# Masking the scores of a causal linear attention: one engine for all 16 heads, or three engines for two halves

## Chip, cores and metric

One core of a Trainium2 chip. The metric is the time of one execution on the device in microseconds (us), the median of several runs.

## What is computed

The program is one transformer-like chain on `x` of 2 x 2048 tokens with 128 channels in float32: a landmark attention, a feed-forward part with blockwise FP4 rounding (FFN), a causal linear attention, and the same FFN again. Each has a layer norm ahead of it and a residual sum behind it. Only the linear attention is touched. Cut to what matters, for 16 heads of 8 channels:

```
q, k = elu(q) + 1, elu(k) + 1
for every token t:                      # a scan over the 2048 tokens
    kv   += k[t] (x) v[t]
    ksum += k[t]
    y[t]  = (q[t] @ kv) / (q[t] . ksum + 1e-6)
out = y @ W_proj + b_proj
```

## The kernel before

The 4096 tokens are 32 tiles of 128 tokens, and four tiles make a quad (`QD = 4`). The scan is done in blocks. In a tile, the part of the same 128 tokens is a product of 128 x 128 scores for each head, masked to the upper triangle, with the values (`lin_scores`, mask, `lin_attend`). The part of all tokens before it comes from a running state of 128 x 128 (`lin_state_mm` on TensorE, `lin_state` on VectorE).

`lin_scores(n)` (line 1488) makes all heads of tile n in four matmuls of 32 rows by 512 columns, one for each group of 32 rows of the array (`r` = 0 to 3), each into a PSUM bank of its own: banks 1 to 4 (`SCORE_BANK = 1`). Banks 1 and 2 hold heads 0 to 7, banks 3 and 4 heads 8 to 15. There is one set of these four banks. The masked scores have two buffers, `masked[n % 2]`.

Before the change the two halves go different ways. VectorE masks heads 0 to 7 straight from PSUM by a product with a triangle of ones (`lin_mask`, line 1091). ScalarE copies heads 8 to 15 out of PSUM unmasked to a buffer `raw` (`lin_raw`, line 698), and POOL, which reads only SBUF in this kernel, selects the triangle from `raw` into `masked` (`lin_select`, line 406). `lin_attend(n)` (line 1507) waits for both halves, and `lin_scores(n + 1)` waits until banks 1 and 2 are masked and, ahead of its third matmul, until banks 3 and 4 are copied out.

Each quad needs front work ahead of its tiles: transposes (`lin_transposes`, 1448), the q and k products (1454, 1455), exponentials (679, 682), caps on POOL (396), the two feature maps on VectorE (`lin_phi`, 1045 and 1049), the v product and the transpose of k, a running sum of k on VectorE (`lin_scan`, 1058), its product with q on POOL (`lin_qk`, 401), the denominators (`lin_den_mms` on TensorE, 1471; `lin_den` on VectorE, 1073 and 1077), their spread (692) and transpose (1478), and the scaled, block-diagonal q on VectorE (`lin_qbd`, 1082 and four instructions of 1085). `lin_scores` of a quad's first tile waits for its `lin_qbd`.

The order is written out by hand. Iteration n of the loop on each engine holds the steps of tile n, the scores and the mask of tile n + 1, and one quarter of the front work of quad q = (n + 1) / 4 + 1, by `phase = (n + 1) % 4`:

- TensorE: scores(n + 1); phase 0 transposes, 1 q and k products, 2 v product, 3 transpose of the denominators; attend(n); state_mm(n); in phase 2 den_mms; proj(n).
- VectorE: out(n - 1); mask(n + 1); stats(n - 1); phase 3 qbd, 1 phi, 2 scan and v; state(n); in phase 2 den.
- ScalarE: raw(n + 1); phase 0 xbT, 1 exps, 2 pk; yT(n); phase 3 norm of the quad after; in phase 2 spread.
- POOL: select(n + 1); phase 1 the caps, 2 qk, 3 bias.

The front work of seven quads (1 to 7) lies in this loop; that of quad 0 lies in the FFN before it. Behind tiles 28 to 31 each engine also does the first steps of the second FFN (`LIN_FILL`: `step1(-4)` to `step1(-1)`). Every engine works its own list in order and stops at a wait.

Of the kernel before, what the change touches and what calls it, by code (L numbers as in the profile page):

```python
# [16 lines left out]
ALU = mybir.AluOpType  # L17
ACT = mybir.ActivationFunctionType
AX = mybir.AxisListType.X

P = 128
B, N = 2, 2048
NT = N // P
TILES = B * NT
# [26 lines left out]
QW = QD * P  # L51
# [6 lines left out]
FRONT_A, FRONT_B, SCORE_BANK, STATE_BANK, NUM_BANK = 7, 0, 1, 5, 6  # L58
# [6 lines left out]
def build(nc, x_d, wqkvT_d, band_d, wfc_d, bfc_d, wattn_d, battn_d, wproj_d, bproj_d,  # L65
          wg_d, wu_d, wd_d, eye_d, scaled_eye_d, tri_d, blockmask_d, headones_d, rowhead_d, valid_d, centre_d, out_d):
    with ExitStack() as ctx:
# [9 lines left out]
        s = Signals()  # L77

        def need(eng, name, value):

            if not (isinstance(value, int) and value <= 0):
                eng.wait_ge(s[name], value)
# [17 lines left out]
        def part(n):  # L100
            used[0] += n
            return arena[:, used[0] - n:used[0]]
# [67 lines left out]
        tri = xn_store[:, 6 * P:7 * P]  # L170
# [7 lines left out]
        phq, phk, kcum, qn = ([part(QW) for _ in range(2)] for _ in range(4))  # L178
        pk = [part(QW).rearrange("p (k c) -> p k c", c=P) for _ in range(2)]
        masked = [part(HB * P).rearrange("p (h t) -> p h t", t=P) for _ in range(2)]  # L180
        raw = part(2 * QW)
        den, rden = (part(QD * HB).rearrange("p (k h) -> p k h", h=HB) for _ in range(2))
        rdenB = part(QW)
        state, ynT = ([part(P) for _ in range(2)] for _ in range(2))
# [2 lines left out]
        ps = ctx.enter_context(nc.psum_tensor("ps", [P, 8, 512], F32))  # L187
        psf = ps[:, :, :].rearrange("p a b -> p (a b)")
# [42 lines left out]
        def lin_states(n):  # L231

            return n - n // NT if n > 0 else 0
# [58 lines left out]
        def _(g):  # L292
            tt = nc.gpsimd.tensor_tensor
# [47 lines left out]
            def layernorm_moments(p, q):  # L341

                g.wait_ge(s["stats_done"], p * TILES + (q + 1) * QD)
                tiles = slice(q * QD, (q + 1) * QD)

                def const(k):
                    return lnc[:, k:k + 1].broadcast_to([P, QD])

                steps = ((0, mv[:, tiles, 1], const(0), ALU.add), (1, ln[:, 0, tiles], const(1), ALU.pow),
                         (2, mv[:, tiles, 0], const(2), ALU.mult), (3, ln[:, 2, tiles], ln[:, 1, tiles], ALU.mult))  # L350
                for k, (o, i0, i1, op) in enumerate(steps):
                    if k in (1, 3):
                        g.wait_ge(s["moment_step"], p * TILES + q * QD + k)
                    tt(out=ln[:, o, tiles], in0=i0, in1=i1, op=op).then_inc(s["moment_step"], 1)  # L354
            for q in range(TILES // QD):
# [3 lines left out]
               op=ALU.add).then_inc(s["band_done"], 1)  # L359
# [4 lines left out]
               op=ALU.mult).then_inc(s["w_quant"], 1)  # L364
# [24 lines left out]
            def lin_bias(q):  # L389
                g.wait_ge(s["lin_xb_done"], q + 1)  # L390
                tt(out=X[:, q * QD:(q + 1) * QD, :], in0=X[:, q * QD:(q + 1) * QD, :],
                   in1=bproj[:, :].unsqueeze(1).broadcast_to([P, QD, P]), op=ALU.add).then_inc(s["lin_bias_added"], 1)
# [7 lines left out]
                need(g, "lin_den_done", q)  # L400
                tt(out=qk, in0=phq[q % 2], in1=kcum[q % 2], op=ALU.mult).then_inc(s["lin_qk_done"], 1)

            def lin_select(n):
                g.wait_ge(s["lin_raw_copied"], n + 1)
                need(g, "lin_num_done", n - 1)
                nc.gpsimd.affine_select(out=masked[n % 2][:, 8:16, :], in_=raw.rearrange("p (h t) -> p h t", t=P),  # L406
                                        pattern=[[0, 8], [1, P]], compare_op=ALU.is_ge, fill=0.0, base=0,
                                        channel_multiplier=-1).then_inc(s["lin_masked_pool"], 1)

            for n in range(TILES):  # L410
                if n % QD == 0 and n > 0:
                    layernorm_moments(1, n // QD - 1)
# [4 lines left out]
            for r in range(PN + 3):  # L417
# [6 lines left out]
                    lin_cap(0, ek, "lin_ek_done", "lin_ek_capped")  # L424
                if r == 16:
                    lin_bias(0)
            lin_select(0)
            layernorm_moments(2, QN - 1)
            lin_bias(1)
            for n in range(TILES):  # L430
                q, phase = (n + 1) // QD + 1, (n + 1) % QD
                if n + 1 < TILES:
                    lin_select(n + 1)
                if q < TILES // QD:
                    if phase == 1:
                        lin_cap(q, eq, "lin_eq_done", "lin_eq_capped")
                        lin_cap(q, ek, "lin_ek_done", "lin_ek_capped")
                    if phase == 2:
                        lin_qk(q)
                    if phase == 3 and q + 1 < TILES // QD:  # L440
                        lin_bias(q + 1)
                if n % QD == 1 and n > QD:
                    layernorm_moments(3, n // QD - 1)
                if n in LIN_FILL:
                    step1(LIN_FILL[n])
# [6 lines left out]
        def _(a):  # L452
            act = nc.scalar.activation
# [238 lines left out]
                act(rdenB.rearrange("p (k h i) -> p k h i", k=QD, i=D), rden.unsqueeze(3).broadcast_to([P, QD, HB, D]),  # L692
                    ACT.Copy).then_inc(s["lin_rden_spread"], 1)

            def lin_raw(n):
                a.wait_ge(s["lin_s23_done"], n + 1)
                need(a, "lin_masked_pool", n)
                act(raw.rearrange("p (a n) -> p a n", a=2), ps[:, SCORE_BANK + 2:SCORE_BANK + 4, :], ACT.Copy).then_inc(s["lin_raw_copied"], 1)  # L698

            def lin_yT(n):  # L700
                a.wait_ge(s["lin_num_done"], n + 1)
                need(a, "lin_proj_done", n - 1)
# [6 lines left out]
            for r in range(PN + 3):  # L709
# [9 lines left out]
                    lin_pk(0)  # L719
                if r == 17:  # L720
                    lin_spread(0)
            lin_raw(0)
            lin_xbT(1)
            for n in range(TILES):
                q, phase = (n + 1) // QD + 1, (n + 1) % QD
                if n + 1 < TILES:
                    lin_raw(n + 1)
                if q < TILES // QD:
                    if phase == 0:
                        lin_xbT(q)  # L730
                    if phase == 1:
                        lin_exps(q)
                    if phase == 2:
                        lin_pk(q)
                lin_yT(n)
                if q + 1 < TILES // QD and phase == 3:
                    lin_norm(q + 1)
                if q < TILES // QD and phase == 2:
                    lin_spread(q)
                if n == 27:  # L740
                    a.wait_ge(s["lin_qn_done"], QN)
                    normalise1(0)
                if n in LIN_FILL:
                    step1(LIN_FILL[n])
# [5 lines left out]
        def _(v):  # L750
            tt, ts, stt = nc.vector.tensor_tensor, nc.vector.tensor_scalar, nc.vector.scalar_tensor_tensor
# [42 lines left out]
            def by_block(t):  # L794
# [25 lines left out]
               op=ALU.subtract).then_inc(s["a2_shifted"], 1)  # L820
# [6 lines left out]
            for c in range(4):  # L827
                k = slice(32 * c, 32 * c + 32)
                last = tt(out=a_bd[k, :, 32 * c:32 * c + 32], in0=a2[k, :, :], in1=a2s[k, 2, :].unsqueeze(2).broadcast_to([32, U, M]),
                          op=ALU.mult)  # L830
# [12 lines left out]
                   op=ALU.max).then_inc(s["a2_chain"], 1)  # L843
# [242 lines left out]
                last.then_inc(s["lin_qbd_done"], 1)  # L1086

            def lin_mask(n):
                v.wait_ge(s["lin_s01_done"], n + 1)
                need(v, "lin_num_done", n - 1)  # L1090
                tt(out=masked[n % 2][:, 0:8, :], in0=psf[:, SCORE_BANK * QW:(SCORE_BANK + 2) * QW].rearrange("p (h t) -> p h t", t=P),  # L1091
                   in1=tri[:, :].unsqueeze(1).broadcast_to([P, 8, P]), op=ALU.mult).then_inc(s["lin_masked_dve"], 1)

            def lin_state(n):
                v.wait_ge(s["lin_state_added"], lin_states(n + 1))
# [67 lines left out]
        def _(pe):  # L1163
# [198 lines left out]
            for u in range(U):  # L1362
                for c in range(4):
                    h = 4 * (u // B) + c
# [116 lines left out]
            def lin_scores(n):  # L1481
                q, k = divmod(n, QD)
                pe.wait_ge(s["lin_qbd_done"], q + 1)
                need(pe, "lin_masked_dve", n)
                for r in range(RG):
                    if r == 2:
                        need(pe, "lin_raw_copied", n)
                    last = mm(ps[:, SCORE_BANK + r, :].rearrange("p (h t) -> p h t", t=P), phk[q % 2][32 * r:32 * r + 32, k * P:(k + 1) * P],  # L1488
                              qbd[q % 2][32 * r:32 * r + 32, :, k * P:(k + 1) * P], start=True, stop=True)
                    if r == 1:  # L1490
                        last.then_inc(s["lin_s01_done"], 1)
                last.then_inc(s["lin_s23_done"], 1)

            def lin_attend(n):
                q, k = divmod(n, QD)
                fresh = n % NT == 0
                need(pe, "lin_x_done", n)
                if not fresh:
                    pe.wait_ge(s["lin_state_copied"], lin_states(n))
                    mm(ps[:, NUM_BANK, 0:P], state[n % 2], qn[q % 2][:, k * P:(k + 1) * P], start=True, stop=False,  # L1500
                       skip_group_check=True)
                pe.wait_ge(s["lin_masked_dve"], n + 1)
                pe.wait_ge(s["lin_masked_pool"], n + 1)
                for j in range(HR):
                    for r in range(RG):
                        w = r * HR * VW + 32 * j
                        last = mm(ps[32 * r:32 * r + 32, NUM_BANK, 0:P], vbd[q % 2][:, k, w:w + 32], masked[n % 2][:, r * HR + j, :],  # L1507
                                  start=fresh and j == 0, stop=j == HR - 1, skip_group_check=True)
                last.then_inc(s["lin_num_done"], 1)
# [103 lines left out]
```

## Time and profile before

| what | value |
|---|---|
| median of 3 runs | 685.26 us (682.94 to 688.97) |
| the profiled execution: time, and span of the core in it | 687.19 us, 685.4 us |
| mean granted TensorE clock (1 is full speed) | 0.942 |
| TensorE matmuls busy | 599.6 us (87%) |
| VectorE busy | 479.8 us (70%) |
| ScalarE busy | 353.5 us (52%) |
| POOL busy | 305.6 us (45%) |

The loop of the linear attention runs from about 407.5 to 585 us of the span. The busy shares are means over stages with different limits; a matmul that waits in the array's pipeline counts as busy. The profile calls VectorE DVE, ScalarE ACT, GpSimd POOL and TensorE PE (its weight loads PEld).

### The profile page before, as it was taken

What the parts mean: (1) busy time and instruction counts of PE and PEld (TensorE: products, weight loads), DVE (VectorE), ACT (ScalarE), POOL (GpSimd) and SP (SyncE); (2) the same over time, 40 slices, a digit from 0 to 9 for tenths busy, and PEclk for the clock granted to TensorE, in tenths of its full rate; (3) what the DMA queues carried; (4) which work ended last, traced back from release to release, by engine and by line L of the source; (5) the groups of instructions that cost most, each with busy time, mean ns of one, the idle gap of its engine ahead of it and who ended that gap; (6) DMA issues with size and microseconds to landing.
All of it is one profiled execution on the core that took longest, in us unless ns stands there. A gap on an engine that the chain in (4) does not pass through costs nothing.

```text
span 685.4 us, 14035 instructions
## 1 busy us (share of the span) xinstructions
PE 599.6 (87%) x5407; PEld 441.1 (64%) x5407; DVE 479.8 (70%) x1015; ACT 353.5 (52%) x652; POOL 305.6 (45%) x353
## 2 busy tenths in 40 slices
PE   3769999799999988979999769898889898699996
PEld 2668888466666677856777655556556564367775
DVE  5455988556666753889998745767667667699972
ACT  4433233244444442269997723444445425699974
POOL 6421111123223322547887554444443434467764
PEclk9688999989999999999999967999999989899999
DMA  9400000000000000000000000000000000000111
GB/s 243 111 2 1 1 2 1 1 1 2 1 2 1 2 22 12 1 0 2 1 1 0 1 0 2 2 1 2 1 1 2 1 2 1 0 17 16 32 32 31
DMA packets 15909, 9.57 MB, mean 14 GB/s; under 512 B 1446, under 2 KB 15718, under 8 KB 15844
## 3 DMA queue, kind: packets, MB, share of 16 engines
q1 hardware_dynamic: 15844, 8.68, 5.0%
q8 instruction: 43, 0.70, 0.4%
q14 instruction: 22, 0.18, 0.1%
HBM read 6.59 MB, written 2.10 MB: 13 GB/s over the span
## 4 chain that ended last, share of the span: by engine, by line
PE 51%; DVE 22%; ACT 10%; POOL 9%; issue 7%; DMA 0%; POOLq 0%; DVEq 0%; ACTq 0%
PE ps L1240 6%; PE ps L1488 5%; PE ps L1380 4%; PE ps L1256 4%; PE ps L1421 3%; PE ps L1397 3%; PE ps L1402 3%; PE ps L1507 3%; DVE r L872 3%; DVE m L912 3%; PE ps L1247 2%; POOL G L313 2%; ACT S L527 2%; DVE arena L1091 2%; ACT qbd L553 2%
## 5 line engine op out<-in xcount | busy, mean ns | idle before, releaser
L371 POOL TENSOR_TENSOR A<-S,r 126x512 f32<-126x512 f32 x36 | 37.7, 1047 | 144.9 <-DVE r L875 132.7
L406 POOL TENSOR_SCALAR_AFFINE_SELECT arena<-arena 128x1024 f32<-128x1024 f32 x32 | 34.9, 1092 | 77.4 <-ACT arena L698 77.4
L313 POOL TENSOR_TENSOR G<-S,hoff 128x704 f32<-128x704 f32 x32 | 48.7, 1521 | 32.1 <-DVE S L1008 30.1
L1397 PE MATMUL ps<-wguT,xnt 128*128 128x352 f32 x128 | 52.0, 489 | 12.0 <-ACT xnt L611 10.6
L1421 PEld LDWEIGHTS ps<-wdT,xnt 128*128 128x128 f32 (+1 forms) x384 | 51.4, 196 | 9.5 <-ACT xnt L618 3.6
L1091 DVE TENSOR_TENSOR arena<-ps,XN 128x1024 f32<-128x1024 f32 x32 | 39.2, 1225 | 26.0 <-PE ps L1488 26.0
L1421 PE MATMUL ps<-wdT,xnt 128*128 128x128 f32 (+1 forms) x384 | 55.0, 281 | 2.6 <-ACT xnt L618 2.6
L698 ACT ACTIVATE arena<-ps 128x1024 f32<-128x1024 f32 x32 | 32.7, 1023 | 40.0 <-PE ps L1488 40.0
L872 DVE TENSOR_REDUCE r<-S 126x16 f32<-126x512 f32 x36 | 24.7, 685 | 32.6 <-ACT S L527 32.6
L1402 PE MATMUL ps<-wguT,xnt 128*128 128x352 f32 x128 | 45.3, 479 | 0.0
L531 ACT ACTIVATE arena<-ps 128x456 f32<-128x456 f32 x36 | 19.9, 552 | 42.4 <-PE ps L1256 42.4
L527 ACT ACTIVATE S<-S 126x512 f32<-126x512 f32 x36 | 22.5, 626 | 34.7 <-DVE S L867 34.7
L990 DVE TENSOR_TENSOR ps<-ps,xnt 128x704 f32<-128x704 f32 x32 | 28.6, 894 | 16.2 <-PE ps L1402 16.2
L1247 PE MATMUL ps<-G,xnt 128*126 128x512 f32 x72 | 39.8, 636 | 0.0
L759 DVE BATCH_NORM_STATS2 stats<-X 128x6 f32<-128x128 f32 x128 | 34.9, 273 | 6.1 <-DMA X<-in_x 4.1
L1256 PEld LDWEIGHTS ps<-band,A 126*32 126x32 f32 x1152 | 28.0, 112 | 15.4 <-issue 7.6
L611 ACT ACTIVATE xnt<-ps 128x352 f32<-128x352 f32 x64 | 29.4, 460 | 16.0 <-PE ps L1397 16.0
L1240 PEld LDWEIGHTS ps<-late 128*128 128x128 f32 x272 | 32.4, 192 | 7.6 <-issue 3.7
L1507 PE MATMUL ps<-arena,early 128*32 128x128 f32 x1024 | 37.0, 289 | 0.0
L1256 PE MATMUL ps<-band,A 126*32 126x114 f32 x1152 | 34.8, 268 | 1.0 <-POOL A L371 1.0
L1240 PE MATMUL ps<-late 128*128 128x128 f32 x272 | 34.0, 278 | 0.6 <-DVE late L884 0.5
L354 POOL TENSOR_TENSOR ln<-ln,lnc 128x4 f32<-128x4 f32 x32 | 32.3, 1011 | 2.5
(202 smaller groups left out, 1529.6 us busy)
## 6 DMA issues: line engine op xcount, KB each, us to landing
X<-in_x SPq DMA_DIRECT2D x8, 256.0 KB, 5.4
out<-X SPq DMA_DIRECT2D x8, 256.0 KB, 2.3
arena<-in_wqkvT SPq DMA_DIRECT2D x4, 256.0 KB, 5.3
band<-in_band SPq DMA_DIRECT2D x1, 897.8 KB
arena<-in_wqkvT SPq DMA_DIRECT2D x1, 512.0 KB, 9.2
early<-in_wfc SPq DMA_DIRECT2D x1, 512.0 KB, 10.4
kI<-in_scaled_eye SPq DMA_DIRECT2D x1, 192.0 KB
XN<-in_wattn SPq DMA_DIRECT2D x1, 192.0 KB, 2.4
```

The lines of the kernel that those rows point to most:

```text
L313: tt(out=hgrid, in0=hmoved[k], in1=hoff[k][:, :], op=ALU.subtract).then_inc(s["fh_grid"], 1)
L371: tt(out=A1v[:, w % NW, :].rearrange("p (h m) -> p h m", m=M), in0=S1v[:, w % NW, :].rearrange("p (h m) -> p h m", m=M), in1=r1[:, 3, w % ...
L527: act(S1v[:, w % NW, :], S1v[:, w % NW, :], ACT.Exp).then_inc(s["s1_exp"], 1)
L872: reduce(out=att1_row(1, w), in_=att1_heads(S1v[:, w % NW, :]), axis=AX, op=ALU.add).then_inc(s["s1_sum"], 1)
L1091: tt(out=masked[n % 2][:, 0:8, :], in0=psf[:, SCORE_BANK * QW:(SCORE_BANK + 2) * QW].rearrange("p (h t) -> p h t", t=P), in1=tri[:, :].uns ...
L1240: last = mm(banks(bank + hf, 1, P)[:, u, :], lhsT[:, 4 * hf + u, :], rhs[:, 4 * hf + u, :], start=True, stop=True)
L1247: mm(ps[0:WI, score_bank(w), :], XNT[:, b, w % WN * WO:w % WN * WO + WI], G1[:, b, :], start=True, stop=True).then_inc(s["s1_done"], 1)
L1256: last = mm(ps[32 * c:32 * c + 32, conv_bank(w), g * WO:(g + 1) * WO], A1v[:, w % NW, h * M:(h + 1) * M], band[:, h, :], start=True, stop= ...
L1397: mm(ps[:, GATE_BANK, 0:F], xT[t // QD % 2][:, t % QD, :], wguT[:, 0:F], start=True, stop=True).then_inc(s["f_gate"], 1)
L1402: mm(up_banks(r)[:, t % 2, :], xT[t // QD % 2][:, t % QD, :], wguT[:, F:2 * F], start=True, stop=True).then_inc(s["f_up"], 1)
L1421: last = mm(ps[:, T_BANK + 1, k * P:(k + 1) * P], hT[r % 2][0:FK[c], k, c, :], wdT[0:FK[c], c, :], start=(c == 0), stop=False)
L1507: last = mm(ps[32 * r:32 * r + 32, NUM_BANK, 0:P], vbd[q % 2][:, k, w:w + 32], masked[n % 2][:, r * HR + j, :], start=fresh and j == 0, st ...
```

## The change

VectorE masks both halves, in two instructions of the same form, one after the other. ScalarE's copy of heads 8 to 15 (`lin_raw`), POOL's select (`lin_select`) and the buffer `raw` are left out. `lin_attend` waits for the one count of masks, and `lin_scores(n + 1)` waits for the first half's mask, and ahead of its third matmul for the second half's. In `lin_scores(n)` of the code after, the counts `2 * n - 1` and `2 * n` stand for the two masks of tile n - 1. Nothing else is moved.

```diff
-            def lin_select(n):
-                g.wait_ge(s["lin_raw_copied"], n + 1)
-                need(g, "lin_num_done", n - 1)
-                nc.gpsimd.affine_select(out=masked[n % 2][:, 8:16, :], in_=raw.rearrange("p (h t) -> p h t", t=P),
...
-            def lin_raw(n):
-                a.wait_ge(s["lin_s23_done"], n + 1)
-                need(a, "lin_masked_pool", n)
-                act(raw.rearrange("p (a n) -> p a n", a=2), ps[:, SCORE_BANK + 2:SCORE_BANK + 4, :], ACT.Copy).then_inc(s["lin_raw_copied"], 1)
...
             def lin_mask(n):
-                v.wait_ge(s["lin_s01_done"], n + 1)
                 need(v, "lin_num_done", n - 1)
-                tt(out=masked[n % 2][:, 0:8, :], in0=psf[:, SCORE_BANK * QW:(SCORE_BANK + 2) * QW].rearrange("p (h t) -> p h t", t=P),
-                   in1=tri[:, :].unsqueeze(1).broadcast_to([P, 8, P]), op=ALU.mult).then_inc(s["lin_masked_dve"], 1)
+                for k in range(2):
+                    v.wait_ge(s["lin_s23_done" if k else "lin_s01_done"], n + 1)
+                    tt(out=masked[n % 2][:, 8 * k:8 * k + 8, :],
+                       in0=psf[:, (SCORE_BANK + 2 * k) * QW:(SCORE_BANK + 2 * k + 2) * QW].rearrange("p (h t) -> p h t", t=P),
+                       in1=tri[:, :].unsqueeze(1).broadcast_to([P, 8, P]), op=ALU.mult).then_inc(s["lin_masked"], 1)
...
-                need(pe, "lin_masked_dve", n)
+                need(pe, "lin_masked", 2 * n - 1)
                 for r in range(RG):
                     if r == 2:
-                        need(pe, "lin_raw_copied", n)
+                        need(pe, "lin_masked", 2 * n)
...
-                pe.wait_ge(s["lin_masked_dve"], n + 1)
-                pe.wait_ge(s["lin_masked_pool"], n + 1)
+                pe.wait_ge(s["lin_masked"], 2 * n + 2)
```

## Rows read from the trace of the kernel before

**Rows 1.** The profile's page, the three instructions for the mask (part 5)

```profile
L406 POOL TENSOR_SCALAR_AFFINE_SELECT arena<-arena 128x1024 f32<-128x1024 f32 x32 | 34.9, 1092 | 77.4 <-ACT arena L698 77.4
L1091 DVE TENSOR_TENSOR arena<-ps,XN 128x1024 f32<-128x1024 f32 x32 | 39.2, 1225 | 26.0 <-PE ps L1488 26.0
L698 ACT ACTIVATE arena<-ps 128x1024 f32<-128x1024 f32 x32 | 32.7, 1023 | 40.0 <-PE ps L1488 40.0
```

**Rows 2.** Windows by quad: stretch, length, busy PE, PEld, DVE, ACT, POOL, clock

```profile
431.00:452.20 21.20, 18.38 (x216) 11.81 (x216) 14.80 (x32) 10.10 (x18) 9.62 (x12) 1.00 0.01 2
...
539.70:563.00 23.30, 21.57 (x220) 14.02 (x220) 14.95 (x32) 8.88 (x15) 9.62 (x12) 0.85 0.01 2
```

**Rows 3.** Timeline, phases 0 and 1, quad after 473.79: start, us, engine, line

```profile
473.79 1.14 PE L1488 MATMUL ps<-qbd,arena 32*128 32x512 f32 x8
...
474.97 1.23 DVE L1091 TENSOR_TENSOR arena<-ps,XN 128x1024 f32<-128x1024 f32 x1 [0.78 <-PE ps L1488]
...
477.61 1.14 PE L1488 MATMUL ps<-qbd,arena 32*128 32x512 f32 x8
...
481.65 0.75 DVE L1045 SCALAR_TENSOR_TENSOR arena<-ps,bias_qk,arena 128x512 f32<-128x512 f32 x1 [1.22 <-POOL arena L396]
```

**Rows 4.** Timeline, phases 2 and 3, quad that starts at 430.96

```profile
441.01 1.23 DVE L1091 TENSOR_TENSOR arena<-ps,XN 128x1024 f32<-128x1024 f32 x1 [0.44 <-PE ps L1488]
...
442.16 0.29 DVE L759 BATCH_NORM_STATS2 stats<-X 128x6 f32<-128x128 f32 x1
442.17 1.09 POOL L406 TENSOR_SCALAR_AFFINE_SELECT arena<-arena 128x1024 f32<-128x1024 f32 x1 [2.85 <-ACT arena L698]
...
442.58 1.75 DVE L1058 TENSOR_TENSOR_SCAN arena<-lnc,arena 128x512 f32<-128x512 f32 x1
...
444.42 1.26 POOL L401 TENSOR_TENSOR arena<-arena 128x512 f32<-128x512 f32 x1 [1.16 <-DVE arena L1058]
...
445.74 1.06 PE L1471 MATMUL ps<-headones,arena 128*128 128x16 f32 x8 [1.58 <-POOL arena L401]
...
447.05 1.14 PE L1488 MATMUL ps<-qbd,arena 32*128 32x512 f32 x8
...
448.23 1.23 DVE L1091 TENSOR_TENSOR arena<-ps,XN 128x1024 f32<-128x1024 f32 x1 [0.43 <-PE ps L1488]
...
449.79 0.67 DVE L1082 TENSOR_TENSOR arena<-ps,arena 128x512 f32<-128x512 f32 x1
...
450.50 1.67 DVE L1085 TENSOR_SCALAR wqkv<-arena,rowhead 128x512 f32<-128x512 f32 x4
...
452.23 1.14 PE L1488 MATMUL ps<-wqkv,arena 32*128 32x512 f32 x8 [1.08 <-DVE wqkv L1085]
```

**Rows 5.** The mask of phase 3 in the quad before 473.79

```profile
469.49 1.23 DVE L1091 TENSOR_TENSOR arena<-ps,XN 128x1024 f32<-128x1024 f32 x1 [0.43 <-PE ps L1488]
```

**Rows 6.** Line 1471 in the loop: durations, and what TensorE and its loads waited for

```profile
L1471 PE MATMUL ps<-headones,arena x56: 262/263/377, 423.6 to 555.9; 128*128 128x16 f32 x56
...
  POOL arena L401: 23.5, 14
```

**Rows 7.** Windows behind the wait of phase 2 in two quads, columns as before

```profile
445.80:449.20 3.40, 3.22 (x27) 2.16 (x28) 1.89 (x4) 1.51 (x2) 1.45 (x4) 1.00 0.00 0
...
489.80:493.20 3.40, 3.40 (x16) 1.74 (x15) 1.96 (x4) 1.65 (x2) 0.38 (x3) 0.51 0.00 0
```

**Rows 8.** Timeline, the scores of phase 3 in the second of them

```profile
489.95 2.09 PE L1488 MATMUL ps<-qbd,arena 32*128 32x512 f32 x8
```

**Rows 9.** Timeline, last tiles with FFN steps

```profile
569.58 0.68 DVE L970 TENSOR_REDUCE xblk<-ps 128x32 f32<-128x512 f32 x1
...
571.50 0.28 DVE L1102 TENSOR_TENSOR X<-ps,X 128x128 f32<-128x128 f32 x1
...
579.09 0.97 DVE L950 TENSOR_SCALAR xblk<-xblk 128x32 f32<-128x32 f32 x1 [0.65 <-POOL A L306]
...
581.10 0.28 DVE L1102 TENSOR_TENSOR X<-ps,X 128x128 f32<-128x128 f32 x1
```

More of the change, by code:

```diff
@@ L180, in build @@
         masked = [part(HB * P).rearrange("p (h t) -> p h t", t=P) for _ in range(2)]
-        raw = part(2 * QW)
         den, rden = (part(QD * HB).rearrange("p (k h) -> p k h", h=HB) for _ in range(2))
@@ L401, in lin_qk @@
                 tt(out=qk, in0=phq[q % 2], in1=kcum[q % 2], op=ALU.mult).then_inc(s["lin_qk_done"], 1)
-            def lin_select(n):
-                g.wait_ge(s["lin_raw_copied"], n + 1)
-                need(g, "lin_num_done", n - 1)
-                nc.gpsimd.affine_select(out=masked[n % 2][:, 8:16, :], in_=raw.rearrange("p (h t) -> p h t", t=P),
-                                        pattern=[[0, 8], [1, P]], compare_op=ALU.is_ge, fill=0.0, base=0,
-                                        channel_multiplier=-1).then_inc(s["lin_masked_pool"], 1)
             for n in range(TILES):
@@ L426, in _ @@
                     lin_bias(0)
-            lin_select(0)
             layernorm_moments(2, QN - 1)
@@ L431, in _ @@
                 q, phase = (n + 1) // QD + 1, (n + 1) % QD
-                if n + 1 < TILES:
-                    lin_select(n + 1)
                 if q < TILES // QD:
@@ L721, in _ @@
                     lin_spread(0)
-            lin_raw(0)
             lin_xbT(1)
@@ L725, in _ @@
                 q, phase = (n + 1) // QD + 1, (n + 1) % QD
-                if n + 1 < TILES:
-                    lin_raw(n + 1)
                 if q < TILES // QD:
```

## The prediction

> **What bounds the kernel now.** I read the costs of the mask first, then the loop quad by quad in windows, then the timeline of each phase with the reason of each wait. The mask costs 1225 ns on VectorE for heads 0 to 7; the other half costs 1023 ns on ScalarE and then 1092 ns on POOL [rows 1]. A quad takes 21.2 to 23.3 us, and in the shortest TensorE is busy for 18.4 us, VectorE for 14.8 and ScalarE and POOL for 10 or less [rows 2]. Read as averages, VectorE has 6.4 us free in a quad and the added masks would fit. The reader is to see that this is the wrong view. The timeline tells which free time is room and which is waiting.
>
> In phases 0 and 1 TensorE is the limit: it goes from one group of scores to the next in 3.82 us (473.79 to 477.61), and VectorE waits for it before its mask [rows 3]. In phases 2 and 3 VectorE's mask stands in a chain that TensorE waits for, twice in each quad [rows 4]:
>
> - Phase 2: mask at 441.01, stats, running sum at 442.58, POOL's product at 444.42, den_mms on TensorE at 445.74 after 1.58 us idle. This wait occurs in all seven quads: 23.5 us for matmuls and weight loads together, 14 times [rows 6].
> - Phase 3: mask at 448.23, stats, qn at 449.79, four instructions of qbd at 450.50, and at 452.23 the scores of the next quad's first tile, before which TensorE idled 1.08 us.
>
> VectorE's free time in phases 2 and 3 lies behind the running sum and behind the denominators, while it waits for the others. Work put ahead of the running sum or of qn can't use it.
>
> **The change part by part.** *The second mask.* One more instruction of the same form for each of 32 tiles. From its predecessor's start to the next start is 442.16 - 441.01 = 1.15 us [rows 4], less than its 1.225 us, as two neighbours overlap. So each costs VectorE 1.15 us, 36.8 us in all. What it costs the program differs by phase.
>
> *Phase 0 and the ones like it.* The mask of 474.97 would end its second half at 474.97 + 1.15 + 1.23 = 477.35, and the scores that overwrite the banks start at 477.61 [rows 3]. 0.26 us are left; VectorE then has stats (0.42 us, 442.16 to 442.58 in [rows 4]), state and out (0.28 us, [rows 9], state alike) to do, and is free at 478.3, before the next scores end at 478.75. Cost nothing, but by a margin of a quarter microsecond; TensorE's own work is what hides it.
>
> *Phase 1.* Phi waited for POOL's cap until 481.65, 1.22 us idle [rows 3]. The second mask takes 1.15 of these. Cost nothing.
>
> *Phase 2.* The running sum, right behind mask and stats with no idle time, moves by 1.15 us, and with it POOL's product, den_mms and everything behind [rows 4]. Seven quads x 1.15 = 8.0 us. TensorE's gap grows from 1.58 to 2.73 us.
>
> *Phase 3.* qn and qbd move by a further 1.15 us. Where the first tile's scores waited for qbd, all of it counts. From mask to those scores it is 4.00 us in four quads (448.23 to 452.23 is one, [rows 4]); in the other three TensorE came later than qbd, and it is 4.30 (469.49 to 473.79, [rows 3, 5]). The new distance is 4.00 + 1.15 = 5.15 everywhere: 4 x 1.15 + 3 x 0.85 = 7.1 us. TensorE's gap here becomes about 1.08 + 1.15 = 2.2 us.
>
> *Wait placed ahead of the third score matmul.* The second half of a tile's banks comes free 1.15 us after the first, not beside it. Ahead of tile 1's scores nothing else lies on TensorE; there it can hold back half the group by up to 1.0 us at the low clock. I take 0.5, bounds 0 and 1.0. Queued behind it on TensorE are the q and k products.
>
> *The last tiles.* VectorE's out of tile 28 at 571.50 comes behind FFN work that began at 569.58, right after a mask and its followers [rows 9]; with a mask more ahead of it it moves by about 1.2 us. The chain then meets POOL's quantising, whose end VectorE awaits at 579.09 and where the select is gone; out of tile 30 (581.10) moves by about 1.1. I take 1.1, bounds 0 and 2.2.
>
> *What is removed.* ScalarE's copy and POOL's select run beside TensorE and VectorE: their end is 1.02 + 1.09 = 2.1 us after the scores, where attend comes one iteration later. In phase 2 select (442.17 to 443.26) is over before the running sum is (444.33), so POOL's product doesn't come earlier [rows 4]. Value nothing, apart from the last tiles, where ScalarE has FFN work queued behind it; that is in the 1.1 above. No DMA or other queue is passed.
>
> One rule would make the removal worth more. Rows 4 show the running sum, which has two SBUF operands, starting at 442.58 while select runs, with 1.75 us as in the other quads. The Trainium skill (page "SBUF — State Buffer", section "Who interferes with whom") says that a VectorE instruction with two SBUF inputs and a GpSimd instruction that reads SBUF contend, and that the second blocks until the first is done. By that rule the sum could not have started before 443.26, and leaving out the select would give back up to 0.68 us in seven quads, 4.8 us. The trace doesn't agree: select takes 1.09 us and the sum 1.75 with their spans overlapping. The sum here goes without it.
>
> *The clock.* TensorE's granted clock falls to half (1.2 of 2.4 GHz) for some 3.4 us behind the wait of phase 2 in six of the seven quads, as at 489.80 (0.51); in one it does not (445.80, 1.00) [rows 7]. It costs where it catches the scores of phase 3, 2.09 us in place of 1.14 [rows 4, 8]: three quads pay it in full and one mostly. In the others it catches work that is hidden behind VectorE's chain. With a gap of 2.73 instead of 1.58 us I expect all seven to fall soon enough to pay: 3.2 us more. The gap of phase 3 grows from 1.08 us, after which no row shows a fall, to 2.2 us, above the 1.58 that mostly brought one. The scores behind it belong to phases 0 and 1, where TensorE is the limit, and 3.4 us at half speed delay it by 1.7. No row has this case. Bounds 0 and 7 x 1.7 = 12; as 2.2 lies nearer to the gaps that brought a fall than to those that didn't, but not every fall meets dense work, I take half, 6 us. So the clock costs 9.2 us, between 0 and 3.2 + 12 = 15, and up to 4 more if den_mms (1.06 us in [rows 4]) ran at half speed each time, some 0.6 us a quad.
>
> *The sum.* 8.0 + 7.1 + 0.5 + 1.1 + 9.2 = 25.9 us on the profiled execution's 687.19, 713. That execution stands 1.9 us above the median of 685.26; from the median it is 711.
>
> **The rivals.** *Hidden (ends on the other side: not slower).* VectorE's 6.4 free microseconds a quad take in the 4 x 1.15 = 4.6, and TensorE at 87% stays the bound. Its place would be phases 2 and 3, and it decides as soon as the running sum and qn can start as early as now, which needs 1.15 us of idle time ahead of them. For it: it is really so in phases 0 and 1. Against it: lines 1058 and 1082 have no idle time before them in rows 4. Time 685.
>
> *Chain without clock.* The two chains grow as worked out, but the clock falls no more often than now: 8.0 + 7.1 + 1.6 = 16.7 us, 702. For it: the falls don't follow the gap's length alone, as one quad shows. Against: the gaps grow by 73% and by a factor of two.
>
> *Heavy clock.* Both gaps bring a fall each time, and den_mms, scores and then phases 0 and 1 pay; the margin of 0.26 us there is also used up. 16.7 + 15 + 4 = 36 at the most, which is 721; the case begins at 30, 715.
>
> *The lock.* The rule above holds after all, and the sum moves 1.15 - 0.68 a quad: 711 - 5 = 706, inside the forecast's range.
>
> *The change doesn't do what it says:* the second mask takes less than the first, since ScalarE no longer reads PSUM beside it. The 512-column forms on VectorE (qn 0.67 us for 512, mask 1.23 for 1024, [rows 4]) lie on one line of about 1.1 ns a column, the former with ScalarE idle, so nothing speaks for it.
>
> **How the numbers follow.** The forecast (706 to 715, both chains and some of the clock) gets 0.52; chain without clock 0.20; heavy clock 0.15; the lock 0.04; hidden 0.07; second mask cheap 0.02. The range reaches from below the second case (699) to the top of the third (720), and holds about 0.85. A measurement of this kernel tells a change from none at about 1%, 7 us. Only the hidden case and a rest fall within it: same 0.07, faster 0.01, slower 0.92.
>
> **What the profile after would show.** Line 1091's successor 64 times at 1225 ns; running sum 2.7 us after the first mask, not 1.57; TensorE's wait for POOL's line 401 near 2.7 us a quad; from mask to the first tile's scores 5.15 us; in phases 0 and 1 still 3.8 us between scores; quads of 23.5 to 26 us with a clock below 0.92. I would be wrong if the waits before den_mms stayed at 1.58 us, if phases 0 and 1 got longer at full clock (the margin was misjudged), or if the clock after the longer gaps stayed full.

## The result and the profile after

The changed kernel takes 714.38 us (median of 4 runs, 710.21 to 716.9) beside 686.21 us of the kernel before on the same chip: a ratio of 1.041, with a 95% interval of 1.033 to 1.048. That is slower by 28 us; 711 us within 699 to 720 was forecast. The profiled execution took 716.9 us, its core's span is 715.1 us, against 687.19 and 685.4.

The page of the kernel after, engines and the costliest group (columns as in [rows 1]):

```profile
PE 615.0 (86%) x5407; PEld 450.6 (63%) x5407; DVE 513.5 (72%) x1047; ACT 322.4 (45%) x620; POOL 272.0 (38%) x321
...
L1073 DVE TENSOR_TENSOR arena<-ps,XN 128x1024 f32<-128x1024 f32 x64 | 75.4, 1219 | 32.4 <-PE ps L1471 32.4
```

The change does what it says: 64 masks of 1.22 us, 34 us more of VectorE and 31 and 34 us less of ScalarE and POOL. (Lines: 1073 mask, 1471 scores, 1454 den_mms, 1039 running sum, 1066 the four of qbd, 390 POOL's bias, 400 POOL's product.) No engine is full, and the program is slower by almost what VectorE gained. By this page alone it would be easy to say that VectorE's load did it. The stages show otherwise. I cut each quad at five instructions, with start times from the timeline, and added up the seven quads:

| from start to start, 7 quads, us | before | after | difference |
|---|---|---|---|
| quad's first scores to the mask of phase 2 | 71.5 | 77.5 | +6.0 |
| that mask to den_mms | 33.1 | 37.9 | +4.9 |
| den_mms to the scores of phase 3 | 10.2 | 14.0 | +3.8 |
| these scores to their mask | 11.7 | 15.2 | +3.5 |
| that mask to the next quad's first scores | 28.9 | 38.9 | +10.0 |
| ahead of the loop's first scores, and behind the start of tile 28's | 530.0 | 531.6 | +1.6 |

The loop of seven quads thus grew from 155.4 to 183.5 us; little changed outside of it.

The timeline of phases 2 and 3 in the second quad of the kernel after (the counterpart of [rows 4]):

```profile
447.95 1.28 DVE L1039 TENSOR_TENSOR_SCAN arena<-lnc,arena 128x512 f32<-128x512 f32 x1
...
449.32 1.26 POOL L400 TENSOR_TENSOR arena<-arena 128x512 f32<-128x512 f32 x1 [5.93 <-DVE arena L1039]
...
450.63 1.89 PE L1454 MATMUL ps<-headones,arena 128*128 128x16 f32 x8 [2.31 <-POOL arena L400]
...
453.07 2.09 PE L1471 MATMUL ps<-qbd,arena 32*128 32x512 f32 x8
...
455.26 2.35 DVE L1073 TENSOR_TENSOR arena<-ps,XN 128x1024 f32<-128x1024 f32 x2 [1.74 <-PE ps L1471]
...
457.95 0.67 DVE L1063 TENSOR_TENSOR arena<-ps,arena 128x512 f32<-128x512 f32 x1
...
458.66 1.68 DVE L1066 TENSOR_SCALAR wqkv<-arena,rowhead 128x512 f32<-128x512 f32 x4
...
460.39 1.68 PE L1471 MATMUL ps<-wqkv,arena 32*128 32x512 f32 x8 [1.45 <-DVE wqkv L1066]
```

By it two forecasts came true: qn starts 2.69 us behind the first mask of phase 3, where it was 1.56 [rows 4], and the scores behind den_mms run at the low clock, 2.09 us in place of 1.14. One was not: the running sum takes 1.28 us, not 1.75. TensorE's gap ahead of den_mms is 2.31 us, not 2.73.

Phase 3 of the fourth quad shows a second thing that was not forecast:

```profile
507.23 2.35 DVE L1073 TENSOR_TENSOR arena<-ps,XN 128x1024 f32<-128x1024 f32 x2 [1.74 <-PE ps L1471]
...
509.89 1.64 ACT L657 ACTIVATE arena<-X,ln 128x128 f32<-128x128 f32 x4
...
510.62 2.68 DVE L1066 TENSOR_SCALAR wqkv<-arena,rowhead 128x512 f32<-128x512 f32 x4
...
511.60 1.42 POOL L390 TENSOR_TENSOR X<-X,XN 128x512 f32<-128x512 f32 x1 [7.35 <-ACT arena L657]
...
513.36 1.14 PE L1471 MATMUL ps<-wqkv,arena 32*128 32x512 f32 x8 [2.83 <-DVE wqkv L1066]
```

The same four instructions of qbd take 2.68 us in place of 1.67, in three of seven quads, and from mask to scores it is 6.13 us there and 5.12 in the others. In the three POOL's bias starts within the four. Two of these three biases are longer themselves (1.50 and 1.42 us in place of 1.27), the third keeps its 1.27. One of the four carries the whole microsecond (at most 1489 ns, median 482):

```profile
L1066 DVE TENSOR_SCALAR wqkv<-arena,rowhead x16: 473/482/1487, 404.4 to 562.7; 128x512 f32<-128x512 f32 x16
L1066 DVE TENSOR_SCALAR qbd<-arena,rowhead x16: 480/481/1489, 432.4 to 590.2; 128x512 f32<-128x512 f32 x16
```

The split of tile 1's scores, and two groups of scores in phases 0 and 1:

```profile
410.67 3.12 PE L1471 MATMUL ps<-wqkv,arena 32*128 32x512 f32 x8 [0.35 <-DVE arena L1073]
...
486.83 1.14 PE L1471 MATMUL ps<-qbd,arena 32*128 32x512 f32 x8 [1.02 <-DVE qbd L1066]
...
490.61 0.71 PE L1471 MATMUL ps<-qbd,arena 32*128 32x512 f32 x4
```

Tile 1 took 3.12 us for its scores, before 2.09: the halves ran one behind the other. In phases 0 and 1 the distance is 3.78 us as before (3.82 in [rows 3]): the second mask is free there. (The last row is cut at the end of the window.) Scores aren't split there, so the margin of 0.26 us held.

### The profile page after: what moved, and what is told of

It reads as the page before. It is cut to its first block, busy times and chain, and to the rows that moved or that the text cites. A ratio compares the mean times of both kernels' runs of the same rounds, so it can differ in the third digit from the quotient of the medians.

```text
span 715.1 us, 13910 instructions
## 1 busy us (share of the span) xinstructions
PE 615.0 (86%) x5407; PEld 450.6 (63%) x5407; DVE 513.5 (72%) x1047; ACT 322.4 (45%) x620; POOL 272.0 (38%) x321
## 4 chain that ended last, share of the span: by engine, by line
PE 49%; DVE 26%; ACT 9%; POOL 8%; issue 6%; DMA 1%; POOLq 0%; SPq 0%; DVEq 0%; ACTq 0%
PE ps L1471 6%; DVE arena L1073 6%; PE ps L1223 6%; PE ps L1363 4%; PE ps L1239 3%; PE ps L1404 3%; PE ps L1380 3%; PE ps L1385 3%; DVE r L853 3%; DVE m L893 2%; PE ps L1489 2%; PE ps L1230 2%; POOL G L312 2%; ACT S L516 2%; ACT qbd L542 2%
## 5 line engine op out<-in xcount | busy, mean ns | idle before, releaser
L1073 DVE TENSOR_TENSOR arena<-ps,XN 128x1024 f32<-128x1024 f32 x64 | 75.4, 1219 | 32.4 <-PE ps L1471 32.4
L1380 PE MATMUL ps<-wguT,xnt 128*128 128x352 f32 x128 | 52.7, 494 | 11.4 <-ACT xnt L600 10.1
L1230 PE MATMUL ps<-G,xnt 128*126 128x512 f32 x72 | 38.9, 622 | 0.0
L1471 PE MATMUL ps<-wqkv,arena 32*128 32x512 f32 x128 | 26.3, 870 | 10.9 <-DVE wqkv L1066 10.5
L1489 PEld LDWEIGHTS ps<-arena,early 128*32 128x32 f32 x1024 | 28.9, 119 | 6.9 <-issue 2.0
```

What stands on the lines that cost most here:

```text
L1073: tt(out=masked[n % 2][:, 8 * k:8 * k + 8, :], in0=psf[:, (SCORE_BANK + 2 * k) * QW:(SCORE_BANK + 2 * k + 2) * QW].rearrange("p (h t) -> p ...
L1230: mm(ps[0:WI, score_bank(w), :], XNT[:, b, w % WN * WO:w % WN * WO + WI], G1[:, b, :], start=True, stop=True).then_inc(s["s1_done"], 1)
L1380: mm(ps[:, GATE_BANK, 0:F], xT[t // QD % 2][:, t % QD, :], wguT[:, 0:F], start=True, stop=True).then_inc(s["f_gate"], 1)
```

## The experiments

Where no other base is named, the edit is to the changed kernel. All were timed beside the kernel before (685.3 to 685.9 us).

**Where the second mask costs.** Two kernels between before and after, complements of each other: `both(n)` says for which tiles VectorE masks both halves.

```diff
+        def both(n):
+            return n % QD in (0, 1)        # the other kernel: (2, 3)
...
             def lin_select(n):
+                if both(n):
+                    return
...
             def lin_raw(n):
+                if both(n):
+                    return
...
+                if both(n):
+                    v.wait_ge(s["lin_s23_done"], n + 1)
+                    tt(out=masked[n % 2][:, 8:16, :], in0=psf[:, (SCORE_BANK + 2) * QW:(SCORE_BANK + 4) * QW]...
```

> The kernel before, with the change made only for tiles whose number leaves 0 or 1 when divided by 4 (their masks fall in phases 0 and 1); the other half of the tiles keeps ScalarE's copy and POOL's select. Theory (two chains): VectorE's second mask is free in phases 0 and 1 apart from the split scores of tile 1 (up to 1 us) and a little at the last tiles; 686 to 690 us, quads as before. Rival (load): VectorE's added work counts wherever it is, half of the instructions give half of the 28 us: 700 us.

> The complement: the change made only for tiles that leave 2 or 3 when divided by 4 (masks in phases 2 and 3). Theory (two chains): nearly the whole loss, 708 to 714 us, with the distance from the mask to the first tile's scores at 5.1 us or 6.1 where POOL's bias runs beside qbd. Rival (load): 700 us.

Measured: 688.94 us (10 runs, ratio 1.0035, interval 1.0015 to 1.0055) for tiles that leave 0 or 1, and 704.53 us (4 runs, ratio 1.028, 1.025 to 1.032) for those that leave 2 or 3. The same 16 instructions cost 3 us in the one place and 19 in the other. The load theory, which gives both the same, falls. The second time lies below the 708 to 714 that I expected. The loop took 156.2 and 173.5 us. In the first, tile 1's scores took 3.12 us, which accounts for 1 of its 3 us. In the second, the distance from mask to first scores was 5.12 us six times and 6.11 once, so POOL's bias met qbd in one quad only, and the clock stayed full behind the wait in two quads; my range had taken both as in the changed kernel. The costs of the halves add up to 22 us, not 28. In the profiled loops they are 0.8 and 18.1 us, where both changes together cost 28.1. Of the 9.2 that are missing, 2 us are the two further quads in which the bias meets qbd, and 6.3 lie in the three rows of the table in which the low clock shows (2.4, 1.4 and 2.5, in their order).

**The running sum and POOL's select.** A select of the same form as before, on spare data, which nobody waits for:

```diff
+            def idle_select(n):
+                g.wait_ge(s["lin_masked"], 2 * n + 2)
+                need(g, "idle_done", n)
+                nc.gpsimd.affine_select(out=spare1..., in_=spare0..., pattern=[[0, 8], [1, P]], compare_op=ALU.is_ge,
+                                        fill=0.0, base=0, channel_multiplier=-1).then_inc(s["idle_done"], 1)
...
                 if n + 1 < TILES:
+                    idle_select(n + 1)
```

> The changed kernel with a POOL select of the same form as the one taken out, on spare data of its own, started for each tile when both its masks are done; nobody waits for it. Theory (shared port): a select that runs beside the running sum lengthens it from 1.28 to 1.75 us as in the kernel before, and the product and den_mms behind it by 0.48 us in each of 7 quads: 3 us slower than the changed kernel, 717 us. Rival (the running sum is shorter for another reason, such as ScalarE's copy being gone or its later place): 1.28 us stays, 714 us.

Measured: 724.52 us, ratio 1.058 (1.055 to 1.060), 10 us above the changed kernel, more than either theory said. The timeline of its phase 2:

```profile
479.35 1.09 POOL L406 TENSOR_SCALAR_AFFINE_SELECT arena<-arena 128x1024 f32<-128x1024 f32 x1 [3.59 <-DVE arena L1086]
...
479.62 1.90 DVE L1052 TENSOR_TENSOR_SCAN arena<-lnc,arena 128x512 f32<-128x512 f32 x1
```

The running sum takes 1.90 us beside the select in six of seven quads. It ends at 481.52, 1.08 us after the select does (480.44). In [rows 4] the same two ends are 444.33 and 443.26, 1.07 us apart, although the sum began at another place in the select. In the one quad where the sum came 0.59 us behind the select's start it took 1.57 us, and again ended 1.07 us after the select. So all but about 0.2 us of the sum's 1.28 comes after the select's end, wherever in the select it began. That is a wait for the select, and not a slower pace beside it, and what is saved without the select is this wait. ScalarE's copy isn't needed for it. The size was missed for two reasons, both read from the same distances as in the table of the stages. From mask to den_mms it is 5.99 us in each quad, 4.0 us more in all. Another 4.0 us lie between a quad's first scores and the mask of phase 2, where the select now ends late ahead of POOL's caps in phase 1, so that VectorE waits 1.37 us for the first of them, which it did not in the changed kernel (10.88 us in place of 10.12 in the quads at full clock). The kernel before has its select some 1.3 us earlier behind the first mask in both phases, so this run shows the effect and not its price there; the price there is read from the two profiles, 1.75 against 1.28 us, 0.47 in each quad.

**qbd and POOL's bias.**

```diff
                     if phase == 3 and q + 1 < TILES // QD:
+                        g.wait_ge(s["lin_qbd_done"], q + 1)
                         lin_bias(q + 1)
```

> The changed kernel, with POOL's bias of phase 3 (two SBUF operands) waiting until the four instructions of qbd are done. Theory (shared port): the four take 1.67 us in all seven quads in place of 2.68 in three of them, and the distance from the phase 3 mask to the first tile's scores is 5.12 in all: 3 us faster than the changed kernel, 711 us. Rival (the extra microsecond in three quads comes from elsewhere): 2.68 us stays in three quads, 714 us.

Measured: 710.16 us (6 runs, ratio 1.035, 1.032 to 1.037), 4 us less than the changed kernel. The four runs of that kernel spread from 710.21 to 716.9, so the time alone doesn't show it; the distances do. In all seven quads qbd takes 1.67 us and mask to scores 5.11 to 5.13. Here is the first, where it was 2.68 us and 6.12 before the wait:

```profile
430.46 1.67 DVE L1067 TENSOR_SCALAR qbd<-arena,rowhead 128x512 f32<-128x512 f32 x4
...
432.19 1.14 PE L1472 MATMUL ps<-qbd,arena 32*128 32x512 f32 x8 [0.81 <-DVE qbd L1067]
...
432.51 1.27 POOL L390 TENSOR_TENSOR X<-X,XN 128x512 f32<-128x512 f32 x1 [8.04 <-ACT arena L658]
```

The extra microsecond comes from the bias that runs beside qbd.

**The clock.** Matmuls that nobody reads, into unused columns of the bank of the numerators, fill TensorE's waits:

```diff
+                if front and phase in (2, 3):
+                    pe.wait_ge(s["lin_yT_copied"], n + 1)
+                    for _ in range(8 if phase == 2 else 6):
+                        mm(ps[:, NUM_BANK, P:2 * P], ynT[n % 2], wproj[:, :], start=True, stop=True)
                 if front and phase == 2:
                     lin_den_mms(q)
                 lin_proj(n)
```

> The changed kernel, with matmuls of 128 x 128 x 128 that nobody reads put into TensorE's waits: 8 ahead of den_mms in phase 2 and 6 ahead of proj in phase 3, behind the copy of the numerators (0.22 us each, 1.8 and 1.3 us, less than the gaps of 2.3 us and, in most quads, of phase 3). They shorten no chain. Theory (clock): the granted clock stays full where it fell in the changed kernel; scores of phase 3 back to 1.14 us, den_mms to 1.06, and 8 to 11 us come back: 703 to 706 us. Rival (the slow stretches follow from something else, or are hidden): 714 us or, by the added work, up to 717.

Measured: 704.92 us (ratio 1.030, 1.026 to 1.033), 9.5 us less, with more work on TensorE. Windows of 24 us from the loop's start, about a quad each (columns as in [rows 2]), and the scores, qbd and bias of phase 3 in its second quad:

```profile
407.00:431.00 24.00, 21.41 (x189) 12.66 (x189) 15.79 (x22) 3.76 (x7) 3.48 (x4) 0.79 0.01 1
431.00:455.00 24.00, 21.61 (x248) 15.03 (x244) 19.52 (x36) 5.85 (x13) 5.52 (x8) 1.00 0.01 2
455.00:479.00 24.00, 21.59 (x248) 14.85 (x240) 19.41 (x36) 5.85 (x13) 5.53 (x8) 1.00 0.01 1
479.00:503.00 24.00, 21.51 (x225) 14.78 (x214) 18.31 (x34) 5.55 (x13) 5.52 (x8) 0.93 0.00 1
```
```profile
452.04 1.14 PE L1471 MATMUL ps<-qbd,arena 32*128 32x512 f32 x8
...
456.68 2.68 DVE L1066 TENSOR_SCALAR wqkv<-arena,rowhead 128x512 f32<-128x512 f32 x4
...
457.20 1.48 POOL L390 TENSOR_TENSOR X<-X,XN 128x512 f32<-128x512 f32 x1 [4.82 <-ACT arena L657]
```

All seven scores groups of phase 3 take 1.14 us and all den_mms 1.06. Low clock is left at the loop's start (0.79 in the first row; tiles 0 and 1 have it in the kernel before too) and in one stretch of the fourth quad. The loop gives back 11.5 us although the bias now meets qbd in six quads instead of three, 3 us more. So the low clock cost the changed kernel about 14.5 us in the loop; the kernel before paid for some of it as well (den_mms to scores and scores to mask in the table, 10.2 and 11.7 us, are 1.0 and 3.0 above the filled kernel's 9.2 and 8.7).

**Both side effects out at once**, by the two edits above together.

> The changed kernel with both side effects taken out: the unread matmuls in TensorE's waits, and POOL's bias behind qbd. What is left of the change is then the two chains alone: the phase 2 chain 1.14 us longer less 0.48 for the shorter running sum (7 x 0.66 = 4.6), the phase 3 chain 1.14 us longer in four quads and 0.8 in three (7.0), the split scores of tile 1 (1.0) and the last tiles (1 to 2). At the clock of the filled kernel, which takes back some 3 us that the kernel before also pays: 697 to 700 us, with all seven distances from mask to first tile's scores at 5.12. Rival (another cost of the change is still unnamed): over 703 us.

Measured: 697.23 us (ratio 1.0155, 1.0124 to 1.0186). The seven distances from mask to scores are 5.11 to 5.13 us, the loop 165.3 us. That is at the lower end of what the named costs give, so no cost of more than 2 or 3 us is unnamed.

**Moving the running sum.** If the chain of phase 2 is the cost, it can be taken off the mask. In phase 1 VectorE already has what the sum needs.

```diff
                 if n > 0:
                     lin_out(n - 1)
+                if q < TILES // QD and phase == 2:
+                    lin_scan(q)
                 if n + 1 < TILES:
                     lin_mask(n + 1)
...
                 if q < TILES // QD and phase == 2:
-                    lin_scan(q)
                     lin_v(q)
```

> The changed kernel with one step of VectorE moved: in phase 2 the running sum stands ahead of the two masks (its input has been ready since phase 1), not behind them. Theory (chains): TensorE no longer waits for den_mms; mask to den_mms falls from 5.4 to about 3.2 us in 7 quads (15.6 us), and with the gap the slow den_mms and phase 3 scores go (up to 7 us): 690 to 698 us. Rival (VectorE's load): the same instructions in another order, over 705 us.

Measured: 701.08 us (ratio 1.024, 1.020 to 1.027), 13 us less, but short of the forecast. From mask to den_mms it is 24.5 us in all in place of 37.9, 13.4 less. Between a quad's first scores and that mask it became 82.8 instead of 77.5, 5.3 more: the sum now holds the mask up by some 0.5 us (10.6 us in place of 10.1), and the low clock reached phases 0 and 1 in the fifth to seventh quads (12.2 to 13.1 us). What is late next ahead of den_mms is the values, which VectorE adds behind the two masks:

```profile
446.06 0.69 DVE L1047 TENSOR_TENSOR early<-ps,XN 128x512 f32<-128x512 f32 x1
...
446.89 1.04 PE L1455 MATMUL ps<-headones,arena 128*128 128x16 f32 x8 [0.92 <-DVE early L1047]
```

The same move to the **kernel before**, and on POOL the product ahead of the select:

```diff
+                if q < TILES // QD and phase == 2:
+                    lin_qk(q)
                 if n + 1 < TILES:
                     lin_select(n + 1)
```

> The kernel before with the same move, and on POOL the product behind the running sum ahead of the select in phase 2. Theory (chains): the 1.58 us gap ahead of den_mms goes in 7 quads (11 us), and most of the slow stretches behind it (3 to 4 us): 671 to 676 us. Rival: ScalarE's spread and VectorE's reciprocal take over and TensorE waits in phase 3 instead: 680 us or more.

Measured: 670.06 us (ratio 0.979, 0.976 to 0.982). The phase 2 of its second quad:

```profile
436.06 1.27 DVE L1058 TENSOR_TENSOR_SCAN arena<-lnc,arena 128x512 f32<-128x512 f32 x1
...
437.26 1.20 DVE L1091 TENSOR_TENSOR arena<-ps,XN 128x1024 f32<-128x1024 f32 x1
437.42 1.29 POOL L401 TENSOR_TENSOR arena<-arena 128x512 f32<-128x512 f32 x1 [2.54 <-DVE arena L1058]
...
438.65 1.10 POOL L406 TENSOR_SCALAR_AFFINE_SELECT arena<-arena 128x1024 f32<-128x1024 f32 x1
...
439.63 1.04 PE L1472 MATMUL ps<-headones,arena 128*128 128x16 f32 x8
```

den_mms follows without a wait, and all scores groups of phase 3 take 1.14 us. The sum is short here too: no select runs beside it. I hadn't counted that, and the time lies 1 us below the expected range.

And with the statistics of phase 3 behind qbd:

```diff
-                if n > 0:
+                if n > 0 and not (q < TILES // QD and phase == 3):
                     lin_stats(n - 1)
                 if q < TILES // QD and phase == 3:
                     lin_qbd(q)
+                    lin_stats(n - 1)
```

> The kernel of the run before, with the layer norm's statistics of phase 3 moved behind qbd on VectorE. Theory: the distance from the phase 3 mask to the first tile's scores falls from 4.0 to 3.6 us where VectorE ends it, up to 0.45 us in each of 7 quads: 668 to 674 us. Rival: TensorE's own work in phase 3 ends it, no change from the run before.

Measured: 668.43 us (ratio 0.975, 0.972 to 0.979), 2.5% faster than the kernel before and the fastest of all. The mask to the next scores fell from 4.0 to 3.77 us, 0.23 where the statistics take 0.42. By the timeline the rest went to a neighbour on POOL once more: qbd now begins while the select runs, and the four take 1.85 us instead of 1.67. No run here tests that.

## Why the prediction was right

The time, the direction and the place were right. Inside the sum phase 2 came out 3.1 us too high and 3.0 us were missing in phase 3; that the two cancel is luck.

*The view of averages.* "The wrong view" stands: 16 masks in phases 0 and 1 cost 3 us, 16 in phases 2 and 3 cost 19.

*Phases 0 and 1 cost nothing.* Right, 3.78 us between scores. What they lose in the table of the stages (6.0 us in its first row) is 1.6 us in the first quad, where tile 1's scores are split, and the clock in the third and seventh quads (1.6 and 2.5 us).

*Phase 2, "seven quads x 1.15 = 8.0 us".* The mask did delay the running sum by 1.13 us, from 1.57 to 2.70 behind the mask. But the sum became 0.47 us shorter, so the chain grew by 0.66 us in a quad: 4.9 us in the table. The step that failed is the one where I set the rule of contention aside, with "The trace doesn't agree: select takes 1.09 us and the sum 1.75 with their spans overlapping" and "The sum here goes without it". In every row of the loop the select ran beside the sum, so 1.75 had no undisturbed row to stand beside; that the spans overlap rules nothing out, since, as the run with the idle select shows, the time spent waiting lies within the sum's own span. The rule of the Trainium skill (page "SBUF — State Buffer", section "Who interferes with whom") was right in kind: the select removed gives back 0.47 us a quad, within the 0.68 of overlap that I had worked out as its limit. The rival called the lock, with a chance of 0.04, was the truth for this term.

*Phase 3, "4 x 1.15 + 3 x 0.85 = 7.1 us".* Measured 7.0 us of chain: 5.12 us everywhere, as said, where the bias keeps away. The same effect in the other direction was not in my sum at all: qbd, moved later, met POOL's bias in three quads and paid 1.0 us in each. The table's 10.0 is 7.0 + 3.0, and the wait ahead of the bias took just these three away. I had looked at VectorE's list and at what waits for it, and not at which POOL instruction it would slide beside.

*The clock, 9.2 us "between 0 and 15".* All seven scores groups of phase 3 did slow down: 3.5 us measured beside 3.2. I took den_mms as unaffected and kept it as a bound of 4; it cost 3.8 more than before (4.8 in five quads, less 1.0 in the seventh, which the kernel before paid). For phases 0 and 1 I took 6 us; the third and seventh quads paid 4.2, and tile 28 behind them 1.5. Together 13.0, beside 9.2 and a bound of 4 for den_mms. The cause is shown by the filled kernel, which has the same chains, more work, the clock at full speed and 9.5 us less time.

*First and last tiles, 0.5 and 1.1.* Tile 1's scores grew by 1.03 us, the upper bound. From the start of tile 28's scores the kernel is 2.0 us longer, within the bound of 2.2, but not for the reason given. From the scores of tile 28 to those of tile 29 it is 4.88 us in place of 3.38, at a clock of 0.67 in place of 1.00: these 1.5 us are the clock, counted above. The step with FFN work that I had priced leaves at most 0.5.

The sum was 8.0 + 7.1 + 1.6 + 9.2 = 25.9. Measured, in the same order: 4.9 for phase 2, 7.0 + 3.0 for phase 3, 1.0 + 0.5 for the first and last tiles and 13.0 for the clock make 29.4 us, where the spans of the two profiled executions differ by 29.7. Of the rivals, "hidden" is ruled out by the two half kernels and "chain without clock" by the filled one. "Heavy clock" would have had a fall behind every wait of phase 3; there were three.

What is left open is why the clock spares one wait and not another. Of the seven waits of the changed kernel ahead of a quad's first scores, those of 2.91, 2.83, 1.02 and 1.00 us were followed by full clock and those of 1.45, 2.68 and 1.73 us by half. The first and the last of them:

```profile
435.13 1.14 PE L1471 MATMUL ps<-qbd,arena 32*128 32x512 f32 x8 [2.91 <-DVE qbd L1066]
...
590.71 2.09 PE L1471 MATMUL ps<-qbd,arena 32*128 32x512 f32 x8 [1.73 <-DVE qbd L1066]
```

So the step of the prediction that went from a longer gap to a likelier fall isn't borne out for these waits, and its 6 us beside 5.7 measured (4.2 + 1.5) is luck too. The runs show that filling the waits prevents most falls, not what decides in between.

## What to carry to other kernels

An instruction that goes from one engine to another costs what it delays behind it on the new one's critical chain, and an engine's free time counts only if it lies ahead of that chain: ask it for each phase of the loop. Where a duration was only ever seen beside a certain neighbour, don't take it as the instruction's own, and when steps slide, list what they will now run beside. The largest gain here came from neither way of masking. In the kernel before, the running sum of phase 2 (and with it POOL's product) taken out of the queue behind the mask and the select was worth 15 us, more than half of what the change lost.

## What the runs showed of the hardware

Two operations of VectorE are longer beside POOL instructions that read SBUF. A running sum over 128x512 took 1.28 us alone, 1.75 beside a select that had begun 0.41 us before it, and 1.90 beside one that had begun 0.27 us before it; in both cases it ended 1.07 to 1.08 us after the select. One of four scalings of 128x512, SBUF to SBUF, took up to 1.49 in place of 0.48 us beside an addition of 128x512 on POOL, and that addition mostly 1.42 to 1.50 in place of 1.27. In the second quad of the changed kernel the addition began only in the last of the four scalings: it took 1.44 us and the four kept their 1.68. The masks, with one operand in PSUM, stayed at 1.20 to 1.23 us in all runs. The second surprise is that TensorE's idle time was dearer than its work: 14 matmuls a quad that nobody reads made the changed kernel 9.5 us faster.
